# Recommendation tower on one core: a shallower order for the first chunks, and the pair spread of a group one chunk sooner

## The chip, the core and the metric

The kernel runs on one core of a Trainium2 chip. The metric is device time in microseconds (us) of one execution. The engines are TensorE (PE, matrix products), VectorE (DVE), ScalarE (ACT), GpSimd (POOL, here the issuer of the table gathers) and SyncE (SP, here the issuer of loads). Each runs its own list of instructions strictly in the written order; they meet through semaphores.

## What is computed

```python
e = stack([tbl_f[ids[:, f]] for f in range(26)], axis=1)      # 512 x 26 x 64, gathered rows
x = layer_norm(dense_t @ Wd.T)                                 # 512 x 128
y = layer_norm(einsum('bnd,ed->bne', e, Ws))                   # per field, over 128
y = layer_norm(einsum('bne,pn->bep', y, Wsi))                  # 26 fields -> 32, over 32
T = concat([x[:, None, :], swapaxes(y, 1, 2)], axis=1)         # 33 vectors of 128
Z = einsum('bnd,bmd->bnm', T, T)[:, TRIL_I, TRIL_J]            # 528 pair products
z = layer_norm(Z @ Wl.T) * mask                                # 512, 384 live
h = relu(concat([z, r_dense_t]) @ W_top1 + b_top1)
h = relu(h @ W_top2 + b_top2)
out = h @ W_top3                                               # 512 x 1
```

All of it is float32.

## The kernel before

The batch of 512 is worked in 4 groups of 128 samples, and a group in 4 chunks of 32, so 16 chunks, numbered n = 4*gp + c. A group needs 13 tiles of gathered rows: 4 in chunk c = 0 and 3 in each other. Every tile takes two indirect gathers on POOL, 104 in all, issued back to back with waits that hold POOL two chunks ahead at most.

One chunk passes through these steps (functions of the code):

1. PE `transpose_rows` writes the gathered rows, transposed, to `ps_gq`; ACT `gt_copy` brings them to SBUF; PE `gram_rows` multiplies by the Gram matrix of the embedding weight, into `ps_gq` again.
2. DVE `variance1` (multiply, reduce), ACT `deviation1` (root), DVE `scale_rows` (reciprocal, scaling of `G`): the first layer norm.
3. PE `project_fields` into `ps_ut`, ACT `ut_copy`, PE `embed` into `ps_y`, DVE `y_evacuate` (adds the bias, into `V`).
4. ACT `square2`, DVE `variance2`, ACT `deviation2`, DVE `normalise2`: the second layer norm, in `V`.
5. PE `pair_products` (16 small products into `ps_z`), ACT `z_evacuate`, DVE `z_merge` (into `zt`).

A finished group is passed on: PE `spread_pairs` (24 tiny moves from `zt` to `ps_z`), ACT `z_copy` (to `zb`, `zx`), PE `project_pairs` (5 matmuls by `wl`, into `ps_tail`), ACT `f_squares`, `deviation3`, `f_scale`, PE `transpose_features`, ACT `zn_copy`, then `layer1`, `layer2`, `layer3` with their evacuations. All of these share `ps_tail`.

The order is written by hand. `slot(n)`, one function for each engine, holds the steps of three chunks that overlap: the transposes of n, the embedding of n-1, the pair products of n-2. In a slot with c == 2, PE spreads the group before, between `gram_rows(n)` and `embed(n-1)`; the embedding of n-1 there must also wait for `normalise2(n-2)`, whose reciprocals lie in the same bank. Chunks 0 to 2 are written out one by one, and from chunk 3 on `slot` runs up to chunk 14. Chunk 15 and the end have an order of their own.

Weight preparation that needs the engines is placed among the first chunks: `prepare_dense` (the dense part of the first top layer, 4 pieces of 2 matmuls), `prepare_b1` (12 matmuls with one column each, for the bias of that layer), `prepare_xsum`, `prepare_last_block` (5 matmuls that complete `wl`), `prepare_means` and `prepare_gains` (ACT passes over `wl`). SP loads `w1d` at once, `w1z` after the gathers of chunk 0, the two parts of `wl` after those of chunks 1 and 2.

Of the kernel before, what the change touches and what calls it, by code (L numbers as in the profile page):

```python
# [31 lines left out]
P = 128  # L32
# [11 lines left out]
DENSE_ORDER = (0, 1, 3, 2)  # L44
# [3 lines left out]
NG = B // GRAN  # L48
# [43 lines left out]
def dlrm_tower(nc, ids_base, table, ws_t, gs_row, ident, small, pair_mask, merge_mask, wsi_rows, span_mask, wsi_small,  # L92
               bs_rep, wd_t, dense_t, wl_blocks, w1_z, w1_d, w2, out):
    with ExitStack() as ctx:
# [3 lines left out]
        def sem(name):  # L98
# [99 lines left out]
         b1_ps, b1_ready, dense_ps, dense_sb, dense_ready, w1_ready, last_in_ready, last_ps, last_mean, last_ready, wl_mean, wl_shift, wl_ready) = [  # L198
# [3 lines left out]
                "x_sd_ready", "x_root", "x_ready", "xsum_ps", "xsum_ready", "b1_ps", "b1_ready", "dense_ps", "dense_sb", "dense_ready",  # L202
# [22 lines left out]
        dense_banks = (ps_tail[:, :], ps_z[:, 1, :])  # L225
# [63 lines left out]
        def _(sp):  # L289
# [51 lines left out]
        def _(act):  # L341
# [9 lines left out]
            def prepare_embedding():  # L351

                act.wait_ge(wc_nat_ps, 1)
                act.copy(wc_nat[:, :], ps_ut[:, 0, 0:P]).then_inc(wc_nat_sb, 1)
                act.wait_ge(bias_ps, 1)
                act.copy(bias_y[:, :], ps_y[:, 0, 0:NPROJ]).then_inc(bias_ready, 1)

            def prepare_x():

                act.wait_ge(xc_ps, 1)  # L360
                act.activation(x_sq[:, :], ps_y[:, 1, :], ACT.Square).then_inc(x_sq_ready, 1)
                act.wait_ge(xvar_ps, 1)
# [14 lines left out]
            def dense_copy(oc):  # L377
                act.wait_ge(dense_ps, DENSE_ORDER.index(oc) + 1)
                act.copy(h1_dense[:, oc, :], dense_banks[oc % 2]).then_inc(dense_sb, 1)

            def dense_bias(oc):

                act.wait_ge(b1_ready, 1)
                act.wait_ge(dense_sb, DENSE_ORDER.index(oc) + 1)
                act.activation(h1_dense[:, oc, :], h1_dense[:, oc, :], ACT.Identity, bias=b1e[:, oc:oc + 1]).then_inc(dense_ready, 1)

            def dense_direct(oc):

                act.wait_ge(dense_ps, DENSE_ORDER.index(oc) + 1)
                act.activation(h1_dense[:, oc, :], dense_banks[oc % 2], ACT.Identity,  # L390
                               bias=b1e[:, oc:oc + 1]).then_inc(dense_sb, 1)
# [131 lines left out]

            def slot(n):
# [5 lines left out]
                if c == 3 and gp > 0:  # L530
# [10 lines left out]
                if c == 2 and gp > 0:  # L541
                    z_copy(gp - 1)
                if c == 3 and gp > 0:
                    f_scale(gp - 1)
                if n == 3:
                    prepare_means(0)
                if n == 4:
                    prepare_gains((0, 1))
# [3 lines left out]
                if c == 1 and gp > 1:  # L552
                    relu2(gp - 2)
                if c == 3 and gp > 0:
# [4 lines left out]
                if c == 1 and gp > 1:  # L559
                    y_copy(gp - 2)  # L560
                if n == 3:
                    prepare_means(1)
                    prepare_last_block()
                if n == 4:
                    prepare_gains((2, 3))
                if n == 5:
                    dense_direct(2)
# [823 lines left out]
```

## Time and profile before

| | us |
|---|---|
| median of 3 runs | 172.6 (172.5 to 173.32) |
| span of the profiled execution, first to last instruction | 170.8 |
| around the span (median less span) | 1.8 |
| PE busy | 149.1 (87%) |
| DVE busy | 125.9 (74%) |
| ACT busy | 82.9 (49%) |
| POOL busy | 100.9 (59%) |

The profiled execution's own time is taken as the median, since only its span is on the page. Busy time is a sum over the whole span. A timeline row gives the start, the duration, the engine, the line of the code, what is written and read, how many instructions were merged, and in brackets the idle time before. Merged matmul rows overlap the next by about 0.1 us, since ends are modelled: the distance of two starts is the safer measure. A float32 matmul is two passes, so `x4` is two matmuls as written.

### The profile page before, as it was taken

Reading aid. Unit: us, or ns where it says so; the run is one execution under the profiler, and the core shown is the slowest. Engines: PE = TensorE matmul, PEld = TensorE weight load, DVE = VectorE, ACT = ScalarE, POOL = GpSimd, SP = SyncE. Lnnn points to the kernel's source line nnn. Section 1 sums busy time; section 2 is a strip of 40 time slices with the busy share of each in tenths; the row PEclk is TensorE's granted clock in tenths of the full one; section 3 lists DMA queues with packets and bytes.
Section 4 is the critical chain, followed back from the end, with each engine's and each line's share of the span. In section 5 each row is a group of like instructions: output and inputs, shape, how many; then the busy total and the mean of one; then the engine's idle time right before and its main releaser. Section 6 shows DMA issues by size and latency. Waiting matters only on the chain.

```text
span 170.8 us, 3523 instructions
## 1 busy us (share of the span) xinstructions
PE 149.1 (87%) x1382; PEld 107.6 (63%) x1382; DVE 125.9 (74%) x262; ACT 82.9 (49%) x220; POOL 100.9 (59%) x109
## 2 busy tenths in 40 slices
PE   0489769997959797999999899999989999898995
PEld 0324458945535656556977565687867566687994
DVE  6596728979819795886599998496998987991044
ACT  3012333328776828776636555553637454552220
POOL 1777777777777777777777777777777200120000
PEclk9999998589996999999999999999999999999999
DMA  4913542615111111111111111111111000000000
GB/s 93 343 24 58 206 124 53 205 37 148 23 31 29 31 25 28 30 23 34 24 27 30 23 31 29 29 25 27 33 23 34 16 0 4 0 4 0 4 0 0
DMA packets 5728, 8.14 MB, mean 48 GB/s; under 512 B 2357, under 2 KB 3279, under 8 KB 5712
## 3 DMA queue, kind: packets, MB, share of 16 engines
q0 software_dynamic: 3328, 3.41, 10.9%
q1 hardware_dynamic: 1664, 3.65, 7.2%
q10 hardware_dynamic: 720, 0.85, 1.5%
q8 instruction: 11, 0.18, 0.5%
q14 instruction: 5, 0.04, 0.1%
HBM read 7.91 MB, written 0.00 MB: 46 GB/s over the span
## 4 chain that ended last, share of the span: by engine, by line
PE 50%; DVE 17%; ACT 12%; POOL 11%; issue 6%; DMA 3%; DVEq 0%
POOL G L331 11%; PE ps_tail L1106 8%; PE ps_y L1057 6%; PE ps_tail L1122 5%; PE ps_gq L1032 4%; PE ps_z L1064 4%; PE ps_ut L1044 4%; DVE V L790 4%; DVE V L774 4%; PE ps_z L1152 3%; PE ps_y L1174 3%; PE ps_tail L1016 3%; ACT sq L437 2%; DVE var L746 2%; DVE var L781 2%
## 5 line engine op out<-in xcount | busy, mean ns | idle before, releaser
L331 POOL DMA_INDIRECT G<-in_table_dram,idx x104 | 98.8, 950 | 34.7 <-issue 31.1
L1044 PE MATMUL ps_ut<-S,G 128*128 128x192 f32 (+4 forms) x128 | 21.8, 316 | 0.4 <-DVE G L760 0.4
L1044 PEld LDWEIGHTS ps_ut<-S,G 128*128 128x128 f32 x128 | 20.1, 199 | 2.0 <-DVE G L760 1.8
L774 DVE TENSOR_TENSOR V<-ps_y,bias_y 128x512 f32<-128x512 f32 x32 | 20.5, 683 | 1.0 <-PE ps_y L1057 0.9
L1064 PEld LDWEIGHTS ps_z<-V 128*64 128x64 f32 x448 | 14.9, 141 | 9.9 <-issue 5.1
L1032 PE MATMUL ps_gq<-gram,gt 128*128 128x128 f32 x104 | 15.9, 293 | 6.0 <-ACT gt L423 5.7
L1057 PE MATMUL ps_y<-ut,wcg 64*128 64x512 f32 x64 | 19.4, 684 | 1.0 <-issue 0.8
L437 ACT ACTIVATE sq<-V 128x1024 f32<-128x1024 f32 x14 | 14.9, 1062 | 10.7 <-DVE V L774 10.7
L781 DVE TENSOR_REDUCE var<-sq 128x32 f32<-128x1024 f32 x14 | 17.1, 1220 | 3.5 <-ACT sq L437 3.3
L1032 PEld LDWEIGHTS ps_gq<-gram,gt 128*128 128x128 f32 x104 | 13.5, 199 | 7.5 <-ACT gt L423 6.5
L1064 PE MATMUL ps_z<-V 128*64 128x67 f32 x448 | 16.9, 229 | 0.1
L428 ACT ACTIVATE sd<-var,eps 128x6 f32<-128x6 f32 (+1 forms) x16 | 4.8, 299 | 20.2 <-DVE var L746 20.2
L742 DVE TENSOR_TENSOR qg<-ps_gq,G 128x384 f32<-128x384 f32 (+1 forms) x16 | 9.4, 586 | 6.6 <-PE ps_gq L1032 6.6
L790 DVE TENSOR_TENSOR V<-V,ps_z 128x1024 f32<-128x1024 f32 x10 | 12.2, 1221 | 0.3
L423 ACT COPY gt<-ps_gq 128x384 f32<-128x384 f32 (+1 forms) x16 | 8.1, 509 | 7.3 <-PE ps_gq L1026 7.3
L1106 PE MATMUL ps_tail<-wl,zb 128*128 128x512 f32 x24 | 11.4, 610 | 0.0
L432 ACT COPY ut<-ps_ut 128x512 f32<-128x512 f32 x16 | 9.4, 584 | 3.2 <-PE ps_ut L1044 2.8
L832 DVE COPY_PREDICATED zt<-mmask,ps_z 128x128 f32<-128x128 int32 x28 | 7.1, 312 | 5.0 <-ACT zt L449 5.0
L337 POOL TENSOR_TENSOR V<-V,r_pool 128x1024 f32<-128x1024 f32 x1 | 1.9, 1920 | 14.7 <-DVE r_pool L796 14.7
L1026 PE MATMUL ps_gq<-eye,G 128*128 128x128 f32 x52 | 9.0, 288 | 1.8 <-DMA G<-in_table_dram,idx 1.8
L1026 PEld LDWEIGHTS ps_gq<-eye,G 128*128 128x128 f32 x52 | 6.3, 145 | 6.5 <-DMA G<-in_table_dram,idx 3.2
L746 DVE TENSOR_REDUCE var<-qg 128x6 f32<-128x384 f32 (+1 forms) x16 | 9.4, 586 | 0.6
(169 smaller groups left out, 236.6 us busy)
## 6 DMA issues: line engine op xcount, KB each, us to landing
G<-in_table_dram,idx POOLq DMA_INDIRECT x104, 2.5
w1z<-in_w_z_dram SPq DMA_DIRECT2D x1, 768.0 KB, 4.3
wl<-in_wl_blocks_dram SPq DMA_DIRECT2D x1, 768.0 KB, 5.3
dns<-in_dense_t_dram ACTq DMA_DIRECT2D x1, 512.0 KB, 4.8
w1d<-in_w_d_dram SPq DMA_DIRECT2D x1, 512.0 KB, 5.2
wl<-in_wl_blocks_dram SPq DMA_DIRECT2D x1, 512.0 KB, 3.6
w2s<-in_w_dram SPq DMA_DIRECT2D x1, 512.0 KB, 3.7
wrow<-in_wsi_rows_dram SPq DMA_DIRECT2D x1, 208.0 KB
```

The lines of the kernel that those rows point to most:

```text
L331: pool.indirect_dma_start(G[:, n // NC, j, g, :], None, table, bass.IndirectOffsetOnAxis(ap=idx[:, k:k + 1], axis=0)).then_inc(gathered[n ...
L437: act.activation(sq2[:, :, :].rearrange("p (b l) q -> p b l q", l=2), chunk_v(n), ACT.Square).then_inc(sq_ready, 1)
L746: dve.reduce_sum(var1[:, 0:2 * count], qg[:, 0:count * P].rearrange("p (t d) -> p t d", d=D), AX_X).then_inc(var1_ready, 1)
L774: dve.tensor_tensor(chunk_v(n)[:, g * CB // 2:(g + 1) * CB // 2, :, :], ps_y[:, g, :].rearrange("p (b l q) -> p b l q", l=2, q=NPROJ), bia ...
L781: dve.reduce_sum(var2[:, :], sq2[:, :, :], AX_X).then_inc(var2_ready, 1)
L790: dve.tensor_tensor(chunk_v(n), chunk_v(n), r2_at(n).rearrange("p (b l) -> p b l", l=2).unsqueeze(3).broadcast_to([P, CB, 2, NPROJ]), ALU. ...
L1026: mm = pe.transpose(ps_gq[:, i * P:(i + 1) * P], G[:, gp, j + i, :, :].rearrange("p g d -> p (g d)"), eye[:, :])
L1032: mm = pe.matmul(ps_gq[:, i * P:(i + 1) * P], gt[:, i * P:(i + 1) * P], gram[:, :], start=True, stop=True)
L1044: mm = pe.matmul(ps_ut[:, chunk % 2, col:col + width], G[:, gp, j, :, :].rearrange("p g d -> p (g d)"), S[:, j, :, :].rearrange("p s q -> ...
L1057: pe.matmul(ps_y[:, g, :], wcg[64 * g:64 * g + 64, :], ut[64 * g:64 * g + 64, :], start=True, stop=True).then_inc(y_ps, 1)
L1064: mm = pe.matmul(z_bank(n)[64 * ct:64 * ct + 64, w, s * SLOTS:(s + 1) * SLOTS], V[:, v, 3:SLOTS], V[:, v, :], start=True, stop=True)
L1106: mm = pe.matmul(ps_tail[:, :], zb[:, k, at] if k < PB else zx[:, at], wl[:, k, :], start=(k == 0), stop=(k == KB - 1))
```

## The change

On every engine chunks 0 to 3 get an order of their own, `early_slot(n)`: a chunk goes through steps 1 to 3 in its own slot rather than over two, with the second layer norm of n-1 and the pair products of n-2 beside it. Chunks 4 and 5 are written out. `prepare_b1` moves from behind the embedding of chunk 0 to ahead of the transposes of chunk 0, and the dense pieces, `prepare_xsum` and the last block (3 and 2 matmuls) lie between `gram_rows(n)` and `project_fields(n)`. The bias is added as the dense pieces leave PSUM, so three passes of `dense_bias` go. `w1z` is loaded ahead of `w1d`, and both parts of `wl` right after the gathers of chunk 0.

Group 0 is spread in chunk 4, behind the pair products of chunk 3, and projected at the end of chunk 5. Groups 1 and 2 are spread at the end of the slot with c == 1 and no longer in that with c == 2; in the slot with c == 1 the pair products of n-2 go ahead of the embedding of n-1, and DVE's `z_merge(n-2)` ahead of `variance2(n-1)`. Chunk 15 and the end are as they were.

```diff
 SP
+            sp.wait_ge(ld_x, 16)
+            sp.dma_start(w1z[:, :, :], w1_z).then_inc(ld_w1z, 16)
             sp.dma_start(w1d[:, :, :], w1_d).then_inc(ld_w1d, 16)
...
 ACT
-            def dense_copy(oc):
...
-            def dense_bias(oc):
...
+            def early_slot(n):
+                gt_copy(n)
+                square2(n - 1)
+                if n == 1:
+                    prepare_means(0)
+                else:
+                    z_evacuate(n - 2)
+                deviation1(n)
+                if n == 1:
+                    dense_direct(1)
+                    prepare_xsum()
+                if n == 2:
+                    prepare_means(1)
+                if n == 3:
+                    prepare_last_block()
+                deviation2(n - 1)
+                ut_copy(n)
+                if n == 3:
+                    prepare_gains((0, 1))
...
             def slot(n):
...
-                if c == 2 and gp > 0:
-                    z_copy(gp - 1)
...
                 deviation1(n)
+                if c == 1:
+                    z_evacuate(n - 2)
                     relu2(gp - 2)
...
                 square2(n - 1)
                 if c == 1:
-                    z_evacuate(n - 2)
                     y_copy(gp - 2)
+                    z_copy(gp - 1)
 DVE
+            def early_slot(n):
+                variance1(n)
+                if n > 1:
+                    z_merge(n - 2)
+                scale_rows(n)
+                variance2(n - 1)
+                if n == 3:
+                    prepare_shift()
+                normalise2(n - 1)
+                y_evacuate(n)
+                x_slots(n)
...
                 x_slots(n - 1)
-                variance2(n - 1)
                 if c == 1:
                     z_merge(n - 2)
+                variance2(n - 1)
...
+            variance2(3)
+            z_merge(2)
+            normalise2(3)
+            variance1(4)
+            scale_rows(4)
+            z_merge(3)
 PE
+            def early_slot(n):
+                transpose_rows(n)
+                if n > 1:
+                    pair_products(n - 2)
+                gram_rows(n)
+                if n == 1:
+                    prepare_dense(1)
+                    prepare_xsum()
+                if n == 2:
+                    prepare_last_block(range(0, 3))
+                if n == 3:
+                    prepare_last_block(range(3, KB))
+                project_fields(n)
+                embed(n)
...
             def slot(n):
...
-                if c == 2 and gp > 0:
-                    spread_pairs(gp - 1)
+                if c == 1:
+                    pair_products(n - 2)
                 embed(n - 1)
...
+                if c != 1:
+                    pair_products(n - 2)
...
+                if c == 1:
                     layer3(gp - 2)
+                    spread_pairs(gp - 1)
...
+            transpose_rows(4)
+            pair_products(2)
+            gram_rows(4)
+            prepare_dense(2)
+            pair_products(3)
+            spread_pairs(0)
+            prepare_dense(3)
+
+            transpose_rows(5)
+            project_fields(4)
+            gram_rows(5)
+            embed(4)
+            project_pairs(0)
```

On PE, chunk 13 (c == 1) before, from the Gram products of chunk 13 to those of chunk 14. `ps_y<-ut,wcg` is the embedding of chunk 12, `ps_z<-V` the pair products of chunk 11, `ps_tail<-h,sm` `layer3`, `ps_gq<-eye,G` the transposes of chunk 14, `ps_z<-zt,eye` the spread of group 2:

```order
L1032 MATMUL ps_gq<-gram,gt 128x128 x2
L1057 MATMUL ps_y<-ut,wcg 128x512 [waits y_sb,ut_sb]
L1064 MATMUL ps_z<-V 64x67 [waits z_merged,v_ready]
L1140 MATMUL ps_tail<-h,sm 1x128 [waits h2_ready]
L1026 MATMUL ps_gq<-eye,G 128x128 [waits q_used,gathered3_2]
L1044 MATMUL ps_ut<-S,G 128x192 [waits ut_sb,g_scaled]
L1032 MATMUL ps_gq<-gram,gt 128x128 [waits gt_sb]
L1152 MATMUL ps_z<-zt,eye 32x4x32 [waits z_merged]
```

The same stretch of the changed kernel:

```order
L1058 MATMUL ps_gq<-gram,gt 128x128 x2
L1090 MATMUL ps_z<-V 64x67 [waits z_merged,v_ready]
L1083 MATMUL ps_y<-ut,wcg 128x512 [waits y_sb,ut_sb]
L1168 MATMUL ps_tail<-h,sm 1x128 [waits h2_ready]
L1180 MATMUL ps_z<-zt,eye 32x4x32 [waits z_merged]
L1052 MATMUL ps_gq<-eye,G 128x128 [waits q_used,gathered3_2]
L1070 MATMUL ps_ut<-S,G 128x192 [waits ut_sb,g_scaled]
L1058 MATMUL ps_gq<-gram,gt 128x128 [waits gt_sb]
```

The pair products stand ahead of the embedding, and the spread, with its wait for the merge, ahead of the transposes, the projection and the Gram products of chunk 14.

On DVE, the changed kernel at chunks 3 to 4, from `variance2(3)` on (`sq` is `variance2`, `zt` a merge, `ps_z<-sd` and `V<-V,ps_z` `normalise2(3)`, `qg` and `var` `variance1(4)`, `G` `scale_rows(4)`, the last merge that of chunk 3, which completes group 0):

```order
L783 TENSOR_REDUCE var<-sq 128x32 [waits sq_ready]
L834 COPY_PREDICATED zt<-mmask,ps_z 128x8x16 [waits z_first]
L790 RECIPROCAL ps_z<-sd 128x32 [waits sd2_ready]
L792 TENSOR_TENSOR V<-V,ps_z 128x16x64 [waits r2_ready]
L744 TENSOR_TENSOR qg<-ps_gq,G 128x512 [waits q_ps]
L748 TENSOR_REDUCE var<-qg 128x8 [waits q_used]
L759 RECIPROCAL ps_y<-sd 128x8 [waits y_sb,sd1_ready]
L762 TENSOR_TENSOR G<-G,ps_y 128x512 [waits r1_ready]
L834 COPY_PREDICATED zt<-mmask,ps_z 128x8x16 [waits z_first]
```

The merge of chunk 3 is last in this list, and the spread of group 0 and the transposes of chunk 5 wait behind it; before, the merge of chunk 3 lay in chunk 5 and the spread in chunk 6.

## Rows read from the trace of the kernel before

**Rows 1.** The page, part 5: the gathers (busy, mean ns, idle before them).

```profile
L331 POOL DMA_INDIRECT G<-in_table_dram,idx x104 | 98.8, 950 | 34.7 <-issue 31.1
```

**Rows 2.** Timeline of POOL, the last gather (start, duration, idle before).

```profile
132.94 0.94 POOL L331 DMA_INDIRECT G<-in_table_dram,idx  x1 [0.30 <-issue]
```

**Rows 3.** Timeline of PE, transposes of chunks 1, 4, 5, 8.

```profile
22.88 0.55 PE L1026 MATMUL ps_gq<-eye,G 128*128 128x128 f32 x3 [1.64 <-DMA G<-in_table_dram,idx]
...
47.96 0.60 PE L1026 MATMUL ps_gq<-eye,G 128*128 128x128 f32 x4
...
56.25 0.55 PE L1026 MATMUL ps_gq<-eye,G 128*128 128x128 f32 x3
...
83.89 0.60 PE L1026 MATMUL ps_gq<-eye,G 128*128 128x128 f32 x4
```

**Rows 4.** Timeline of PE, chunks 13 and 14, and chunk 15's transposes.

```profile
125.27 1.13 PE L1057 MATMUL ps_y<-ut,wcg 64*128 64x512 f32 x4
126.44 1.16 PE L1064 MATMUL ps_z<-V 128*64 128x67 f32 x32
...
128.87 0.55 PE L1026 MATMUL ps_gq<-eye,G 128*128 128x128 f32 x3
129.39 1.33 PE L1044 MATMUL ps_ut<-S,G 128*128 128x192 f32 x8
...
131.61 1.41 PE L1152 MATMUL ps_z<-zt,eye 64*32 64x128 f32 x48
133.32 1.13 PE L1057 MATMUL ps_y<-ut,wcg 64*128 64x512 f32 x4 [0.29 <-issue]
...
138.14 0.49 PE L1026 MATMUL ps_gq<-eye,G 128*128 128x128 f32 x3
```

**Rows 5.** Timeline of DVE, chunk 13.

```profile
127.36 1.28 DVE L774 TENSOR_TENSOR V<-ps_y,bias_y 128x512 f32<-128x512 f32 x2
...
129.25 0.18 DVE L768 COPY V<-x_sb 128x32 f32<-128x32 f32 x1
129.77 1.22 DVE L781 TENSOR_REDUCE var<-sq 128x32 f32<-128x1024 f32 x1 [0.34 <-ACT sq L437]
130.91 0.51 DVE L832 COPY_PREDICATED zt<-mmask,ps_z 128x128 f32<-128x128 int32 x2
```

**Rows 6.** Timeline of PE: dense projection, `prepare_b1`, last block, a dense piece, `layer1`.

```profile
8.34 3.56 PE L975 MATMUL ps_y<-dns,wd 128*128 128x512 f32 x4
...
26.62 3.49 PE L988 MATMUL ps_tail<-sm,w1z 128*128 128x1 f32 x24
...
43.56 4.56 PE L1016 MATMUL ps_tail<-wl,dmat 128*128 128x512 f32 x10
...
62.31 1.98 PE L1006 MATMUL ps_tail<-dns,w1d 128*128 128x512 f32 x4
...
81.11 2.94 PE L1122 MATMUL ps_tail<-zn,w1z 128*128 128x128 f32 x24
```

**Rows 7.** The page, part 6: KB and us to landing of two loads.

```profile
w1z<-in_w_z_dram SPq DMA_DIRECT2D x1, 768.0 KB, 4.3
...
dns<-in_dense_t_dram ACTq DMA_DIRECT2D x1, 512.0 KB, 4.8
```

**Rows 8.** Windows: us, then PE, PEld, DVE, ACT, POOL busy, PEclk, DMA.

```profile
28.00:30.00 2.00, 2.00 (x14) 2.00 (x13) 1.53 (x4) 1.06 (x1) 1.70 (x2) 0.66 0.19 33
30.00:32.00 2.00, 1.82 (x8) 1.73 (x9) 1.93 (x12) 0.70 (x2) 1.39 (x3) 0.50 0.54 77
```

**Rows 9.** Timeline of DVE, scaling of chunk 15.

```profile
142.18 0.56 DVE L760 TENSOR_TENSOR G<-G,r 128x384 f32<-128x384 f32 x1
```

**Rows 10.** Timeline of ACT, `square2(12)`.

```profile
128.67 1.06 ACT L437 ACTIVATE sq<-V 128x1024 f32<-128x1024 f32 x1 [0.38 <-DVE V L774]
```

**Rows 11.** Timeline of DVE, `normalise2(2)` and `variance1(4)`'s product.

```profile
52.13 1.22 DVE L790 TENSOR_TENSOR V<-V,ps_z 128x1024 f32<-128x1024 f32 x1
53.27 0.68 DVE L742 TENSOR_TENSOR qg<-ps_gq,G 128x512 f32<-128x512 f32 x1
```

More of the change, by code:

```diff
@@ L529, in slot @@
                     deviation2(n - 2)
-                if c == 3 and gp > 0:
+                if c == 3:
                     f_squares(gp - 1)
@@ L557, in slot @@
                 if c == 1:
-                    z_evacuate(n - 2)
-                if c == 1 and gp > 1:
                     y_copy(gp - 2)
[L561 to L567, printed above, removed]
-                    prepare_gains((4,))
-                if n == 6:
-                    dense_bias(0)
-                    dense_bias(1)
-                if n == 7:
-                    dense_bias(3)
+                    z_copy(gp - 1)
             prepare_embedding()
             prepare_x()
-            dense_copy(0)
-            dense_copy(1)
             gt_copy(0)
             deviation1(0)
-            dense_copy(3)
-            gt_copy(1)
+            dense_direct(0)
             ut_copy(0)
-            deviation1(1)
-            square2(0)
-            gt_copy(2)
-            deviation2(0)
-            ut_copy(1)
-            deviation1(2)
-            square2(1)
-            prepare_xsum()
-            for n in range(3, NCHUNK - 1):
+            for n in range(1, NC):
+                early_slot(n)
+            square2(3)
+            gt_copy(4)
+            z_evacuate(2)
+            deviation2(3)
+            prepare_gains((2, 3))
+            deviation1(4)
+            z_evacuate(3)
+            dense_direct(2)
+            prepare_gains((4,))
+            z_copy(0)
+            dense_direct(3)
+            gt_copy(5)
+            ut_copy(4)
+            deviation1(5)
+            square2(4)
+            for n in range(6, NCHUNK - 1):
                 slot(n)
@@ L912, in _ @@
             prepare_x_root(1)
-            prepare_x()
+            prepare_b1()
             variance1(0)
             scale_rows(0)
+            prepare_x()
             dve.wait_ge(x_ready, 1)
             x_slots(0)
-            variance1(1)
-            dve.wait_ge(bias_ready, 1)
+            prepare_last_block()
             y_evacuate(0)
-            scale_rows(1)
-            variance2(0)
-            prepare_b1()
-            prepare_last_block()
-            for n in range(2, NCHUNK - 1):
+            for n in range(1, NC):
+                early_slot(n)
+            variance2(3)
[4 more added lines that the diff above has]
+            z_merge(3)
+            variance1(5)
+            y_evacuate(4)
+            scale_rows(5)
+            x_slots(4)
+            variance2(4)
+            for n in range(6, NCHUNK - 1):
                 slot(n)
```

104 lines of the change are left out of this document (41 added, 63 removed).

## The prediction

> **What bounds the kernel now.** I read the gathers on POOL first, then the transposes on PE against them, then one steady chunk on all engines.
>
> The 104 gathers take 950 ns each and 31.1 us of issue between 102 of them, 0.30 each, so one every 1.25 us without a real hold [rows 1]. The last one starts at 132.94 [rows 2], and with about 2.4 us from start to landing (1.0 of issue left over, estimate from chunk 1: its sixth gather, number 14, starts at 132.94 - 90 x 1.25 = 20.4, and PE goes on at 22.88 when it lands [rows 3]) chunk n's rows are there at 20.4 + 2.4 + 1.25 x (gathers behind the 14th): chunk 4 at 47.8, chunk 5 at 55.3, chunk 8 at 80.3, chunk 13 at 120.3, chunk 14 at 127.8, chunk 15 at 135.3. PE's transposes start at 47.96, 56.25, 83.89, 128.87 and 138.14 [rows 3, 4]. So up to chunk 4 the gathers pace the kernel within 0.2 us, and from there on PE is late by 1 to 4 us: it is bound by its own work and by the loop through DVE and ACT. The most that any order can win without touching the end is therefore the 2.8 us by which chunk 15 is late (138.14 against 135.3). Behind chunk 15's transposes the code is unchanged and lasts 170.8 - 138.14 = 32.7 us.
>
> In all that follows, what counts is when the transposes of a chunk start, since each slot hangs on them. I write T4 for the start of chunk 4's.
>
> **The steady slots, c == 1 and c == 2 (chunks 9, 10 and 13, 14).** Before, in chunk 13: embedding of 12 at 125.27, pair products of 11 at 126.44 (they wait for `normalise2(11)`, the embedding does not), then T14 at 128.87, projection 129.39, spread 131.61, embedding of 13 at 133.32 [rows 4]. The spread filled a time in which PE would have waited: the embedding of 13 waits for `normalise2(12)` anyway, and 0.29 of idle remains ahead of it.
>
> After, step by step:
> - The pair products still start at 126.44 (same wait), and the embedding of 12 now stands behind them: 126.44 + 1.09 = 127.53, 2.26 later than before.
> - `y_evacuate(12)` starts when the first half has left PE, 1.13 after the start of the embedding (its length in rows 4): 128.66 instead of 127.36 [rows 5], 1.3 later.
> - From its start to the end of `x_slots` 129.25 + 0.18 - 127.36 = 2.07 [rows 5], so the merge of 11, now next, can start at 130.7 and takes 0.5: the spread can start at 131.2. (That ACT has the group's last `z_evacuate` ready by then follows from the pair products ending at 127.5; in rows 5 it came only behind `variance2`.)
> - The spread takes 1.4 [rows 4], so T14 is at 132.6 instead of 128.87: +3.7.
> - From T14 to the embedding of 13 it is 133.32 - 128.87 = 4.45 [rows 4]. The spread that lay in there was cover, not cause: the path is transposes, projection, `ut_copy`, `deviation2(12)`, `normalise2(12)`. ACT does `z_copy` ahead of `gt_copy(14)`, which moves the Gram products by less than the projection hides. So the 4.45 stay, and the embedding of 13 is +3.7 too; pair products and group projection follow it at once, and T15 inherits it.
>
> This is once for group 1 (T8 to T12) and once for group 2 (T12 to T15): 2 x 3.7 = 7.4. The bounds: if the merge came at once after the pair products the spread would only move 1.4 forward and back, 0; if all of the spread and its waits came on top, 131.61 + 1.4 against 128.87 gives 4.1 each, 8.2. I take 3.7, which is a chain of named rows.
>
> **Chunk 4, written out.** From T4 to T5 it is 8.3 before (56.25 - 47.96 [rows 3]). After, T5 stands behind the spread of group 0 and a dense piece, and the spread behind the whole second layer norm of chunk 3: evacuation of 3 (0.06 + 1.28, [rows 5]), `square2(3)` 1.06 [rows 10], `variance2(3)` 1.22 and the merge of 2 about 0.5 [rows 5], `normalise2(3)` 0.38 + 1.22, `variance1(4)` 2 x 0.68 [rows 11], the root of chunk 4 0.3, `scale_rows(4)` 0.95 (estimate from 0.56 for three tiles in rows 9 and a reciprocal), the merge of 3 0.5, spread 1.4, dense piece 1.85 [rows 4, 6]: 12.0 with semaphore steps of 0.02. That is +3.7. DVE is the path here, with PE idle two times; `gt_copy(4)` is also queued behind `square2(3)` on ACT.
>
> **Chunks 5 to 7.** T5 to T8 is 27.6 before (83.89 - 56.25 [rows 3]). After: chunk 5 takes transposes 0.45, projection 1.55, Gram 0.9, embedding 1.07, group projection 4.5 (five matmuls like the last block's 4.56 [rows 6]) = 8.45. Then 4.45 to the embedding of 5, the same path as above [rows 4]. From there the loop is the evacuation 1.13 + 1.28, `square2` 1.06, `variance2` 1.22, roots and `f_squares` 1.35, `gt_copy(7)` 0.5, Gram 0.9, embedding 1.07, feature transposes 0.5, pair products 1.1, `layer1` 2.9 (the small ones are estimates, the rest is in [rows 4, 5, 6, 10]) = 13.0. Sum 25.9, so -1.7 of the possible 3.4 (spread 1.41 and dense piece 1.98 are gone from here [rows 4, 6]); the rest is lost because ACT has `f_squares` and `gt_copy(7)` behind `square2(5)`. Bounds -3.4 and 0. Chunks 4 to 7 together: +2.0.
>
> **Chunks 0 to 3.** The dense projection starts at 8.34 and lasts 3.56 [rows 6]; now it waits only for its own data, which land 4.8 us after an issue at about 2.15 [rows 7], so at 7.0: 1.3 sooner. The variance matmul ends at 12.4. `w1z` is issued at 7.0 and lands 4.3 us later [rows 7], in time. Then `prepare_b1` stands between this and T0: 3.5 us [rows 6], so T0 is near 15.9. Chunk 0 must now be embedded ahead of T1. From transposes to scaled rows takes 4.6 in chunk 15 (138.14 to 142.18 + 0.56 [rows 4, 9]); four tiles and ACT's queue make it 5.3; projection and copy 2.2, embedding 1.07: T1 at 24.5. Before it was 22.88, bound by the gathers.
>
> To this comes the clock. PE's granted clock fell to 0.66 in the stretch from 28 us and 0.50 in that from 30 us, right behind the 24 one-column passes of `prepare_b1` (26.62 for 3.49) [rows 6, 8], though PE counted as busy for 2.00 of 2.00 us. Half is 1.2 instead of 2.4 GHz. The same block now stands ahead of chunk 0's transposes, Gram products and first dense piece, on the path, where I expect the same fall: twice 0.4 + 1.1 and, of the dense piece, 0.8 beyond what DVE hides, so +2.3 and T1 at 26.8. Before, the slow stretch lay in the wait for chunk 2's and 3's gathers and cost nothing later. The bounds of this term are 0 and 3.5 (rows 6 and 8 allow all of 3.5 us of path at half speed to be doubled).
>
> The Trainium skill has, in "TensorE: Matmul & The Clock Gate", Part 1, that a monitor of how busy the array has been sets the clock, and that activity lifts the throttle. Taken by its word, a block that counts as busy should keep the clock up, and the time would be that of the second rival below; the trace speaks against it.
>
> From T1 to T4 three early slots follow. Each is one chain: 4.6 to the scaled rows, projection 1.05, `ut_copy` 0.6, embedding 1.07, 7.4 in all, and to it what ACT and DVE have ahead in their queues: the passes over `wl` ahead of `deviation1`, the last block's 3 x 0.9 us on PE ahead of `project_fields(2)` [rows 6], its evacuation ahead of `ut_copy(3)`, and `variance2(n-1)` with its root ahead of every `ut_copy(n)` (1.22 [rows 5]). I put 1.0 for these, 8.4 each, 25.2 for three; with 7.4 it would be 22.2. The gathers bring a chunk every 7.5 us, so this order gives no lead back. T4 = 26.8 + 25.2 = 52.0 against 47.96: +4.1. Bounds: T4 can't be earlier than 47.8 (-0.2).
>
> On queues: the same page says that ACT and DVE work strictly in order while PE may pull a weight load ahead. That is what makes `gt_copy(4)` wait behind `square2(3)`; no number above hangs on it beyond the rows.
>
> SP's moved loads (`wl` right behind chunk 0's gathers, 1280 KB) run beside chunk 1's gathers. Before, `w1z` did the same beside chunk 1's. I cost them at 0, up to 1 us if chunk 1's rows land late, which the later T1 hides. The three `dense_bias` passes that go from ACT cost 0.7 each in chunks 6 and 7, off the path: 0.
>
> **Sum.** +4.1 (chunks 0 to 3) + 2.0 (chunks 4 to 7) + 7.4 (groups 1 and 2) = +13.5 us on the span, 184.3; with 1.8 around it 186.1 us, against the median of 172.6.
>
> **Rivals.**
> - *The change does what it could* (faster). The early order finishes its backlog in the gathers' shadow, chunk 7 starts when its rows are there, and the moved spread lets chunks 14 and 15 do so too: T15 = 135.3, and the time 135.3 + 32.7 + 1.8 = 169.8. For it: PE is late by 1 to 4 us everywhere from chunk 5 on, and a slot c == 2 gets 1.4 us shorter on PE. Against it: DVE is busy to the last tenth in chunk 13 and the merge can't come sooner. It decides if the spread follows `layer3` with less than 0.3 us of wait. 0.11.
> - *Only the steady slots lose.* The early chunks keep T8 at 83.9, since the clock doesn't fall and the early slots take 7.5: 172.6 + 7.4 = 180.0; with the early slots as summed and only the clock kept up, 186.1 - 2.3 = 183.8. Together 0.22.
> - *The clock falls again and again.* PE idles in the new chunk 13 for 1.2 ahead of the pair products, 1.8 ahead of the spread and 1.5 ahead of the embedding of 13. A slow stretch like that at 28 to 32 us in a place where PE is the path costs up to 2 us; one for each of two groups gives 190. 0.10.
> - *Nothing comes through.* Later waits take up all shifts: 172.6 within 0.5%. Against it: chunks 13 to 15 have no slack on PE in rows 4. 0.03.
>
> The forecast, 186.1 with both the clock and the queues as above, has 0.54. Its own range is 182 to 188.
>
> A measurement of this kernel tells 0.5% (0.9 us) from no change. Faster by more 0.11, within 0.03, slower 0.86. The range, 8 in 10, takes in the second and third rival and leaves the first out: 177 to 190.
>
> **What would show it.** T1 near 26.8, T4 near 52, T5 12 us behind T4, T8 near 90; in chunks 9 and 13 an idle time of over 1 us ahead of the spread, ended by `z_merge`, and T14 over 7 us behind the embedding's place of before; granted clock 0.5 near 15 to 21 us. Wrong I am if the spread starts right behind `layer3`, or if T8 is at or before 83.9, or if slots of the early chunks take 7.5 us.

## The result and the profile after

The changed kernel takes 188.33 us (187.88 to 189.56, 4 runs) against 172.96 (172.5 to 173.53, 4 runs): ratio 1.0905, 95% interval [1.0865, 1.0945]. It is 9% slower; forecast were 186.1, in a range of 177 to 190. The profiled execution has a span of 187.8 us. It is 17.0 longer than that of before, while the medians differ by 15.4: the profiled execution, 189.56 us, is the slowest of the four, and the next part shows a reason why executions of such a kernel differ by 2 us at the start. Here and below medians and ranges are of all executions, while a ratio with its interval goes by the fast ones alone, so it can differ from the quotient of the two medians.

From the page of the changed kernel: span, busy time by engine, and PE's granted clock in 40 slices of 4.7 us:

```profile
span 187.8 us, 3522 instructions
...
PE 154.9 (83%) x1382; PEld 111.0 (59%) x1382; DVE 125.6 (67%) x262; ACT 81.6 (43%) x217; POOL 100.5 (54%) x109
...
PEclk9999999999999999987999976999999999999999
```

The work is the same (1382 matmul passes); the idle time grew by 11.2 us (21.7 to 32.9), and PE's busy time by 5.8 us for the same passes; the trace shows stretches at half clock as the reason. The line of the clock shows falls near 84, 108 and 115 us, but none at the start; that it leaves one out is seen below.

Timeline of PE in the changed kernel, the transposes of chunks 1, 4, 5, 8 and 15 (T1, T4, T5, T8, T15), which answer to [rows 3] and the last row of [rows 4]:

```profile
28.52 0.55 PE L1052 MATMUL ps_gq<-eye,G 128*128 128x128 f32 x3
...
52.78 0.66 PE L1052 MATMUL ps_gq<-eye,G 128*128 128x128 f32 x4
...
64.78 0.49 PE L1052 MATMUL ps_gq<-eye,G 128*128 128x128 f32 x3
...
91.14 0.60 PE L1052 MATMUL ps_gq<-eye,G 128*128 128x128 f32 x4
...
155.16 0.49 PE L1052 MATMUL ps_gq<-eye,G 128*128 128x128 f32 x3
```

| stretch | before | after | difference | forecast |
|---|---|---|---|---|
| start to T4 | 47.96 | 52.78 | +4.8 | +4.1 |
| T4 to T5 | 8.3 | 12.0 | +3.7 | +3.7 |
| T5 to T8 | 27.6 | 26.4 | -1.3 | -1.7 |
| T8 to T12 | 31.9 | 38.2 | +6.3 | +3.7 |
| T12 to T15 | 22.3 | 25.8 | +3.5 | +3.7 |
| T15 to the end | 32.7 | 32.6 | 0 | 0 |

(T12 starts at 115.83 before and 129.36 after.)

Timeline of PE in chunks 13 and 14 of the changed kernel, to be read against [rows 4]: pair products of 11, embedding of 12, `layer3`, spread, T14, embedding of 13.

```profile
139.97 1.16 PE L1090 MATMUL ps_z<-V 128*64 128x67 f32 x32 [1.21 <-DVE V L792]
141.06 1.13 PE L1083 MATMUL ps_y<-ut,wcg 64*128 64x512 f32 x4
142.35 0.60 PE L1168 MATMUL ps_tail<-h,sm 128*1 128x128 f32 x4 [0.16 <-ACT h L480]
144.78 1.41 PE L1180 MATMUL ps_z<-zt,eye 64*32 64x128 f32 x48 [1.83 <-DVE zt L834]
146.13 0.55 PE L1052 MATMUL ps_gq<-eye,G 128*128 128x128 f32 x3
...
150.34 1.13 PE L1083 MATMUL ps_y<-ut,wcg 64*128 64x512 f32 x4 [1.74 <-issue]
```

The two idle times are there: 1.21 ahead of the pair products, 1.83 ahead of the spread, ended by the merge (`zt`), and a third of 1.74 ahead of the embedding of 13, which [rows 4] has as 0.29. T13 to T14 takes 10.37 us instead of 6.65. The same chunk on DVE (evacuation of 12, merge of 11), against [rows 5]:

```profile
142.22 1.29 DVE L776 TENSOR_TENSOR V<-ps_y,bias_y 128x512 f32<-128x512 f32 x2 [1.25 <-PE ps_y L1083]
...
144.22 0.51 DVE L834 COPY_PREDICATED zt<-mmask,ps_z 128x128 f32<-128x128 int32 x2
```

The evacuation waits 1.25 for the embedding that was put behind, and starts 6.46 behind T13 (135.76) instead of 5.14 (127.36 - 122.22), 1.3 later; 2.0 after its start comes the merge at 144.22, and the spread 0.56 behind it. The step-by-step sum of the prediction gave these as 1.3, 2.0 and 0.5.

Chunk 4 on DVE in the changed kernel (evacuation and `variance2` of 3, `normalise2(3)`, merge of 3), and PE beside it (pair products of 3, spread of group 0):

```profile
52.88 1.29 DVE L776 TENSOR_TENSOR V<-ps_y,bias_y 128x512 f32<-128x512 f32 x2 [0.17 <-PE ps_y L1083]
...
55.29 1.22 DVE L783 TENSOR_REDUCE var<-sq 128x32 f32<-128x1024 f32 x1 [0.83 <-ACT sq L430]
...
57.30 1.22 DVE L792 TENSOR_TENSOR V<-V,ps_z 128x1024 f32<-128x1024 f32 x1
...
61.06 0.51 DVE L834 COPY_PREDICATED zt<-mmask,ps_z 128x128 f32<-128x128 int32 x2
```

```profile
58.60 1.16 PE L1090 MATMUL ps_z<-V 128*64 128x67 f32 x32
61.62 1.41 PE L1180 MATMUL ps_z<-zt,eye 64*32 64x128 f32 x48 [1.87 <-DVE zt L834]
```

DVE's chain runs from 52.88 to the merge at 61.06, with waits for ACT of 0.83 and 0.37 in it, and PE idles 1.87 for it. The spread starts 8.84 behind T4; the prediction's terms ahead of it add up to 8.83.

### The profile page after: what moved, and what is told of

It reads as the page before. It is cut to its first block, busy times and chain, and to the rows that moved or that the text cites. A ratio compares the mean times of both kernels' runs of the same rounds, so it can differ in the third digit from the quotient of the medians.

```text
span 187.8 us, 3522 instructions
## 1 busy us (share of the span) xinstructions
PE 154.9 (83%) x1382; PEld 111.0 (59%) x1382; DVE 125.6 (67%) x262; ACT 81.6 (43%) x217; POOL 100.5 (54%) x109
## 4 chain that ended last, share of the span: by engine, by line
PE 61%; DVE 19%; ACT 10%; issue 6%; DMA 2%; ACTq 1%; DVEq 0%
PE ps_y L1083 9%; PE ps_tail L1134 7%; PE ps_z L1090 6%; PE ps_gq L1058 5%; PE ps_ut L1070 5%; PE ps_tail L1150 5%; DVE V L776 4%; DVE var L783 4%; PE ps_z L1180 3%; ACT sq L430 3%; PE ps_tail L1031 3%; PE ps_gq L1052 3%; DVE V L792 3%; PE ps_tail L1012 3%; PE ps_y L1202 3%
## 5 line engine op out<-in xcount | busy, mean ns | idle before, releaser
L1070 PE MATMUL ps_ut<-S,G 128*128 128x192 f32 (+4 forms) x128 | 21.7, 315 | 1.6 <-DVE G L762 1.6
L1058 PE MATMUL ps_gq<-gram,gt 128*128 128x128 f32 x104 | 16.8, 305 | 4.7 <-ACT gt L416 4.6
L1090 PEld LDWEIGHTS ps_z<-V 128*64 128x64 f32 x448 | 15.1, 142 | 8.8 <-DVE V L792 5.1
L1058 PEld LDWEIGHTS ps_gq<-gram,gt 128*128 128x128 f32 x104 | 14.3, 209 | 5.9 <-ACT gt L416 4.6
L792 DVE TENSOR_TENSOR V<-V,ps_z 128x1024 f32<-128x1024 f32 x11 | 13.4, 1221 | 0.4
L1083 PEld LDWEIGHTS ps_y<-ut,wcg 64*128 64x128 f32 x64 | 5.1, 192 | 11.3 <-issue 7.2
L1180 PE MATMUL ps_z<-zt,eye 64*32 64x128 f32 (+1 forms) x192 | 5.7, 346 | 5.5 <-DVE zt L834 5.5
```

The costliest lines, as they stand in the source:

```text
L792: dve.tensor_tensor(chunk_v(n), chunk_v(n), r2_at(n).rearrange("p (b l) -> p b l", l=2).unsqueeze(3).broadcast_to([P, CB, 2, NPROJ]), ALU. ...
L1058: mm = pe.matmul(ps_gq[:, i * P:(i + 1) * P], gt[:, i * P:(i + 1) * P], gram[:, :], start=True, stop=True)
L1070: mm = pe.matmul(ps_ut[:, chunk % 2, col:col + width], G[:, gp, j, :, :].rearrange("p g d -> p (g d)"), S[:, j, :, :].rearrange("p s q -> ...
L1083: pe.matmul(ps_y[:, g, :], wcg[64 * g:64 * g + 64, :], ut[64 * g:64 * g + 64, :], start=True, stop=True).then_inc(y_ps, 1)
L1090: mm = pe.matmul(z_bank(n)[64 * ct:64 * ct + 64, w, s * SLOTS:(s + 1) * SLOTS], V[:, v, 3:SLOTS], V[:, v, :], start=True, stop=True)
L1180: return pe.matmul(dst[32 * q:32 * q + 32, ct, :, 32 * i:32 * i + 32], eye[half, 32 * qb:32 * qb + 32], rows, start=True, stop=True)
```

## Where the start loses: a clock that the profile doesn't always record

Timeline of PE in the changed kernel, from the dense projection to the first dense piece: projection, variance matmul, `prepare_b1`, T0, Gram products of 0, dense piece 0; then the window of 14 to 16 us (busy time of PE, PEld, DVE, ACT and POOL, then the granted clock):

```profile
6.79 3.75 PE L999 MATMUL ps_y<-dns,wd 128*128 128x512 f32 x4 [1.01 <-DMA dns<-in_dense_t_dram]
...
11.23 2.07 PE L1004 MATMUL ps_z<-x_sq,ones 128*128 128x512 f32 x2
13.10 5.12 PE L1012 MATMUL ps_tail<-sm,w1z 128*128 128x1 f32 x24
18.07 1.09 PE L1052 MATMUL ps_gq<-eye,G 128*128 128x128 f32 x4
19.94 2.05 PE L1058 MATMUL ps_gq<-gram,gt 128*128 128x128 f32 x8 [0.77 <-ACT gt L416]
21.77 3.55 PE L1031 MATMUL ps_tail<-dns,w1d 128*128 128x512 f32 x4
```

```profile
14.00:16.00 2.00, 2.00 (x11) 2.00 (x11) 1.94 (x2) 0.03 (x1) 1.62 (x2) 1.00 0.37 53
```

The granted clock reads 1.00, but the matmuls here take almost twice their time: the dense piece 3.55 us instead of 1.88, the variance matmul 2.07 instead of 1.12, T0's transposes 1.09 instead of 0.60. `prepare_b1` takes 5.12; the 3.49 of before [rows 6] was itself partly at half clock ([rows 8]: its last 2 us lie in the stretch of 0.66), and by experiment 3, where a third of it takes 0.95, the whole block at full clock would be some 2.9 (estimate). So PE ran at 1.2 GHz up to about 25 us in this execution. The dense projection is slow in every profile, that of before included: 3.42 to 3.78 us for as many passes as the dense piece does in 1.88, the record at 1.00. What differs is whether PE is faster behind it. In the profile of experiment 4, with the same code up to here, the variance matmul and `prepare_b1` are faster, and a fall of the clock is recorded while the block runs:

```profile
11.25 1.13 PE L1004 MATMUL ps_z<-x_sq,ones 128*128 128x512 f32 x2 [0.35 <-ACT x_sq L363]
12.21 3.75 PE L1012 MATMUL ps_tail<-sm,w1z 128*128 128x1 f32 x24
```

```profile
13.00:14.00 1.00, 1.00 (x10) 1.00 (x9) 0.87 (x1) 0.10 (x1) 0.69 (x2) 0.86 0.04 10
14.00:16.00 2.00, 2.00 (x11) 2.00 (x11) 2.00 (x2) 0.00 (x0) 1.57 (x2) 0.50 0.38 59
```

There T0 is at 15.82 and T1 at 26.00; in the changed kernel's profile they are at 18.07 and 28.52. The forecast was 15.9 and 26.8. (That the dense projection starts at 6.8 to 7.1 instead of 8.34 has one more reason in the code: the change also puts the small bias matmul of `prepare_bias`, which waits for DVE, behind it.) So the start costs 2.5 us more or less by the clock at which PE enters this code, at a place that is now on the path to the end. Before, that place was not on the path: all runs of the kernel before lie within 171.3 and 174.0, while three experiments that keep this start spread over 6 to 7 us and experiment 2, with the same start, over 3 (the changed kernel's own four lie within 1.7). Only one execution of each is profiled, so how much of that spread is the start isn't shown; between the two profiles above it is 2.5.

The Trainium skill, "TensorE: Matmul & The Clock Gate", Part 1, warns that the trace's clock events on this chip can be unreliable. The trace here agrees: 1.00 in the row, double durations beside it.

## Experiments

Each is compared with runs of the kernel before on the same chip: 172.8 us for experiments 1 to 4, 173.5 for 5 and 172.6 for 6 to 8. Times are medians, with the ratio's interval.

**1. The steady slots alone, in the kernel before.**

```diff
 PE, slot(n), groups 2 and 3
-                if c == 2 and gp > 0:
+                if c == 2 and gp == 1:
                     spread_pairs(gp - 1)
+                if c == 1 and gp > 1:
+                    pair_products(n - 2)
                 embed(n - 1)
...
                     layer3(gp - 2)
+                    spread_pairs(gp - 1)
 ACT
-                if c == 2 and gp > 0:
+                if c == 2 and gp == 1:
                     z_copy(gp - 1)
...
+                    z_evacuate(n - 2)      # ahead of relu2
...
+                    z_copy(gp - 1)         # behind y_copy
 DVE
+                if c == 1 and gp > 1:
+                    z_merge(n - 2)         # ahead of variance2
```

> The kernel before with only the steady part of the change, in chunks 9, 10, 13 and 14: pair products ahead of the embedding, merge ahead of variance2, spread at the end of the slot with c == 1. Theory (each move is paid where it stands, the losses add): chunk 9 to 10 and 13 to 14 take 10.4 us instead of 6.65, as in the changed kernel, so +3.7 twice less 0.2 each, +7 us: 179.6, with idle times of 1.2 and 1.8 ahead of the pair products and the spread; if the granted clock falls once as it did in group 1 of the changed kernel, 182.2. Rival (the steady slots only lose because the early order brings them late and out of step): within 1 us of before, 172.5 to 173.5.

Measured: 181.99 (181.54 to 182.8), ratio 1.0526 [1.0464, 1.0589]. T9 to T10 and T13 to T14 both take 10.36. T8 stands at 83.43, T8 to T12 takes 36.8 and T12 to T15 26.9. The windows behind the two spreads show the clock:

```profile
100.00:102.00 2.00, 2.00 (x20) 1.93 (x12) 0.00 (x0) 1.33 (x3) 1.39 (x3) 0.50 0.09 17
138.00:140.00 2.00, 2.00 (x10) 2.00 (x10) 0.00 (x0) 0.90 (x3) 0.08 (x1) 0.50 0.09 16
```

So the steady slots are paid where they stand, 3.5 a group, and with a fall of the clock in both groups 1.4 and 1.1 more. That the early order brings them out of step is refuted.

**2. The early order alone: the changed kernel with the steady slots of before.**

> The changed kernel with its steady slots (from chunk 9 on) put back to the order before; the early order stays. Theory (losses add): T8 at 91.1 as in the changed kernel, then 31.9 a group as before: 188.3 - 6.3 - 3.5 = 178.5. Rival (late and out of step): the early order is the cause of the later losses, and the time stays above 185. Second rival (PE, now late, catches up in the gathers' slack): below 176.

Measured: 177.38 (175.75 to 178.69), ratio 1.0171 [1.0099, 1.0243]. T8 at 89.62, then 31.93 for T8 to T12 and 22.31 for T12 to T15, within a hundredth what the kernel before takes. The losses add, and nothing is caught up afterwards: 4.6 for the early order and 9.2 for the slots make 13.8 of the 15.4. By the ratios it is 3.0 and 9.1. So 1.6 to 3.6 of the whole stays open, where this kernel's own runs differ by 2.9. Part of what they differ by is the clock again: in this profile it fell behind the spread of group 0, where PE had idled 1.87, and T4 to T5 took 13.6 instead of 12.0.

**3. A third of `prepare_b1`.** Its loop over k runs once, so two thirds of that bias sum are missing.

```diff
                 for oc in range(OC1):
-                    for k in range(LLIVE):
+                    for k in range(1):
...
```

> The changed kernel with 4 of the 12 one-column matmuls of prepare_b1 (two thirds of the sum for the first layer's bias are left out). In the changed kernel they take 5.0 us from 13.1 and stand ahead of chunk 0's transposes. Theory (this block and the slow PE behind it are the path until chunk 4): T0 comes 3.3 us sooner, T4 too, and the end 3.3 us, 185.0; up to 1 more if PE runs at full speed sooner. Rival (the gathers or DVE's reciprocals of x set T0 and chunk 0's chain): T0 is at 17.5 or so and the time falls by less than 1.

Measured: 185.58 (183.16 to 190.04); with such a spread the median says little, the trace more:

```profile
11.99 0.95 PE L1012 MATMUL ps_tail<-sm,w1z 128*128 128x1 f32 x8
15.13 1.08 PE L1052 MATMUL ps_gq<-eye,G 128*128 128x128 f32 x4 [2.19 <-DMA G<-in_table_dram,idx]
```

The block took 0.95 us, and then PE waited 2.19 for the gathers of chunk 0: T0 can't be before 15.1. Against 18.07 that is 2.9 sooner, but against the execution of experiment 4 (15.82) only 0.7. T4 is at 49.55, T8 at 86.41. So what `prepare_b1` costs ahead of T0 depends on the clock at which PE enters it: some 2.9 where PE is slow from the start (a third of the 5.12 would end at 14.8 there, still ahead of the gathers; estimate), and where it isn't, the gathers hide all but 0.7. Both theories were half right. The Gram products behind it still took 2.05, and the clock fell at the same place as with the whole block, though the third had ended at 12.94 and PE stood idle:

```profile
13.00:14.00 1.00, 0.00 (x0) 0.00 (x0) 1.00 (x1) 0.00 (x0) 0.70 (x2) 0.65 0.17 33
```

In all three profiles that record a fall at this start (experiments 2, 3 and 4) it comes between 13 and 14 us. That speaks against the one-column passes as its cause; what the cause is stays open.

**4. The idle time ahead of the spread filled, in the changed kernel.**

```diff
-            def layer3(gp):
+            def layer3(gp, times=1):
...
-                for k in range(OC2):
+                for k in list(range(OC2)) * times:
...
                 if c == 1:
-                    layer3(gp - 2)
+                    layer3(gp - 2, 4)
                     spread_pairs(gp - 1)
```

> The changed kernel with layer3 issued four times over in chunks 9 and 13 (1.5 us more of PE work with the same result), which fills most of the 1.82 us in which PE idles ahead of the spread. Theory (that idle time costs nothing by itself, and with it filled the granted clock doesn't fall in group 1, where the changed kernel lost 2.6 us): 188.3 - 2.6 = 185.7, chunk 9 to 10 still 10.4. Rival (the clock falls for another reason, or by chance of phase): 188.3 or a fall at another place. Rival (PE work is the bound): +1.5 twice, 191.

Measured: 185.34 (182.98 to 189.18), ratio 1.0704 [1.0596, 1.0813]. `layer3`, spread of group 1 and the embedding of 9:

```profile
100.35 1.91 PE L1168 MATMUL ps_tail<-h,sm 128*1 128x128 f32 x16 [0.16 <-ACT h L480]
102.77 1.41 PE L1180 MATMUL ps_z<-zt,eye 64*32 64x128 f32 x48 [0.52 <-DVE zt L834]
...
108.32 1.13 PE L1083 MATMUL ps_y<-ut,wcg 64*128 64x512 f32 x4 [1.74 <-issue]
```

```profile
PEclk9995799999999999789999999999999999999999
```

1.3 us more of PE work cost nothing: T9 to T10 takes 10.36. The idle time ahead of the spread is 0.52, and no slice of group 1 or 2 shows a fall. T8 to T12 takes 35.4, where the changed kernel took 38.2. This is one execution, the fastest of the four (182.98 us); the slowest, not profiled, took 6.2 more. Of the 6.6 us by which its span is shorter than the changed kernel's, 2.8 lie in group 1 and 2.5 ahead of T4, so the two times alone don't tell what the filling is worth. The changed kernel's windows in group 1:

```profile
108.00:110.00 2.00, 2.00 (x8) 2.00 (x9) 0.00 (x0) 1.32 (x3) 1.62 (x2) 0.50 0.16 32
114.00:116.00 2.00, 2.00 (x24) 1.13 (x22) 1.39 (x3) 0.30 (x1) 1.40 (x2) 0.50 0.13 25
```

**5. The same filling with the slots alone,** to tell cause from chance (experiment 1 with the `layer3` of experiment 4).

> The kernel before with the steady part of the change, as in the first of these experiments (span 179.7, T8 to T12 36.8 us, T12 to T15 26.9, granted clock down to 0.7 in both groups), and layer3 issued four times over in chunks 9 and 13, which fills the idle time ahead of the spread with 1.5 us of PE work of the same result. Theory (the two idle times of a slot let the granted clock fall, and that is what the groups lose beyond 3.5 each): no fall in the two groups, T8 to T12 35.4 and T12 to T15 25.8 as in the changed kernel with the same filling, the end 2.5 sooner, 179.5. Rival (the filled kernel of before kept its clock by chance of phase): the fall stays, 182; rival (PE work is the bound): 185.

Measured: 179.8 (179.51 to 182.2), ratio 1.0411 [1.0323, 1.0499].

```profile
PEclk9999998799999999999999978999999999999999
```

The embedding of 9, and the window behind it:

```profile
103.68 1.13 PE L1061 MATMUL ps_y<-ut,wcg 64*128 64x512 f32 x4 [1.74 <-issue]
```

```profile
105.00:107.00 2.00, 2.00 (x33) 1.87 (x28) 1.86 (x5) 0.87 (x1) 1.60 (x2) 0.50 0.22 40
```

Group 2 behaved as expected: T12 to T15 takes 25.8, without a fall. Group 1 didn't: the clock fell and T8 to T12 took 37.0. It fell in another place than in experiment 1, though: there at 100 us, behind the spread, here at 105 us, behind the 1.74 of idle time ahead of the embedding, which was left unfilled. So the expectation was half wrong.

All profiles together say more than a pair of them. In the five with the spread at c == 1 and no filling (the changed kernel and experiments 1, 3, 6 and the second of 7) there are ten such spreads in groups 1 and 2, with 1.8 or 2.5 of idle time ahead: the clock fell within 1.5 us of the spread's start at six of them. In the two with the filling (0.5 of idle time) it fell at none of four. Behind the idle time ahead of the embedding (1.3 to 1.9) it fell at four of fourteen. In the four profiles with the spread at c == 2 (the kernel before, experiments 2 and 8 and the first of 7) it fell nowhere in these groups. So no fall in these groups came without an idle time of 1.6 or more just ahead of it, but the same idle time was followed by a fall at one place and not at the next, and how much of it is needed stays open.

**6. Chunk 5's transposes ahead of group 0's spread, in the changed kernel.**

```diff
 ACT
+            gt_copy(5)
+            ut_copy(4)
             z_copy(0)
             dense_direct(3)
-            gt_copy(5)
-            ut_copy(4)
...
 PE
             pair_products(3)
-            spread_pairs(0)
-            prepare_dense(3)
-
             transpose_rows(5)
             project_fields(4)
             gram_rows(5)
+            spread_pairs(0)
+            prepare_dense(3)
             embed(4)
```

> The changed kernel with chunk 5's transposes, chunk 4's projection and chunk 5's Gram products ahead of group 0's spread and the last dense piece, as the order before has it: PE works while DVE runs variance1(4), scale_rows(4) and the merge of 3. Theory (chunk 4 costs 3.7 because PE stands 1.87 ahead of the spread; the projection of 4 can't start before 8.35 behind T4 either): T5 comes 7.1 instead of 12.0 behind T4, but T6 only 0.9 sooner, the end 0.9 sooner, some 187 against 188.3. Rival (the spread's place is the whole loss of chunk 4): T6 and the end 3.7 sooner, 184.6.

Measured: 186.22 (183.64 to 190.23), ratio 1.068 [1.0563, 1.0797].

```profile
60.46 0.55 PE L1052 MATMUL ps_gq<-eye,G 128*128 128x128 f32 x3
61.97 1.63 PE L1070 MATMUL ps_ut<-S,G 128*128 128x160 f32 x10 [0.97 <-DVE G L762]
...
72.97 0.49 PE L1052 MATMUL ps_gq<-eye,G 128*128 128x128 f32 x3
```

T5 is 6.9 behind T4 (53.55), T6 19.4 instead of the 20.0 of the changed kernel and of experiments 3 and 4. The projection of 4 waits 0.97 for DVE's scaling and starts 8.42 behind T4, where 8.35 was expected. So moving the spread back alone wins 0.6 in T4 to T6, and there the rival's 3.7 is refuted: most of chunk 4's loss is DVE's chain with all of PE's work hung behind it, not one place in PE's list. The whole time can't decide this: the runs spread over 6.6 us, and two of the four, 183.6 and 184.9, are as short as the rival had it.

**7. The exchange alone, and the spread alone, in the kernel before.** Of experiment 1's edit, first only `pair_products` ahead of `embed` with its evacuation and merge, the spread left in c == 2:

> The kernel before with only the exchange in the slots with c == 1 of groups 2 and 3: pair products ahead of the embedding, z_merge ahead of variance2; the spread stays in c == 2. Theory: the embedding of 12 comes 2.3 later, the evacuation behind it 1.3, the scaled rows of 13 too, and the path through the projection of 13 loses 1.25 a group: 172.8 + 2.5 = 175.3. Rival (the exchange is what makes the slot 10.4 long): 180.

Measured: 175.12 (173.95 to 175.91), ratio 1.0166 [1.0078, 1.0254]. Embedding of 12, T14 and the projection of 13:

```profile
127.59 1.13 PE L1060 MATMUL ps_y<-ut,wcg 64*128 64x512 f32 x4
...
129.41 0.55 PE L1029 MATMUL ps_gq<-eye,G 128*128 128x128 f32 x3
130.79 1.33 PE L1047 MATMUL ps_ut<-S,G 128*128 128x192 f32 x8 [0.83 <-DVE G L761]
```

T14 is 7.12 behind T13 instead of 6.65, the projection of 13 waits 0.83 for the scaled rows, and T12 to T15 takes 23.65, +1.3. Then only `spread_pairs` and `z_copy` moved:

> The kernel before with only the spread (and z_copy) moved from c == 2 to the end of the slot with c == 1 in groups 2 and 3, behind a z_merge that still follows variance2. Theory (what costs is that PE waits for a merge which DVE gives only at the end of its slot): the merge ends at 131.4 in chunk 13 of before, T14 at 132.8 instead of 128.87, +3.9 a group: 180.6, about that of both parts together. Rival (without the exchange the spread is nearly free): 173 to 175.

Measured: 182.33 (181.93 to 182.63), ratio 1.0567 [1.0477, 1.0658]. The spread of group 2:

```profile
136.27 1.41 PE L1153 MATMUL ps_z<-zt,eye 64*32 64x128 f32 x48 [2.52 <-DVE zt L833]
```

It waits 2.52 for a merge that comes behind `variance2`, and T13 to T14 takes 10.58. So the spread at the end of c == 1 costs 3.9 by itself, as expected. The time is 1.7 above the expected 180.6, since the clock fell in both groups here too: T8 to T12 takes 37.0 and T12 to T15 27.3, which is 5.1 and 5.0 more than before. The exchange shortens its wait (1.8) but costs 1.3 elsewhere, and together they cost 3.7: the exchange gives back only 0.2.

**8. A version that beats both.** The change's aim was to have less waiting among the first chunks. In the kernel before PE waited there for ACT: `gt_copy(4)` queued behind the passes over `wl`. Only these passes are moved:

```diff
 ACT, slot(n)
+                if n == 6:
+                    prepare_gains((2, 3))
+                    prepare_gains((4,))
...
-                if n == 4:
-                    prepare_gains((0, 1))
+                if n == 4:
+                    prepare_last_block()
+                if n == 5:
+                    prepare_gains((0, 1))
...
                 if n == 3:
                     prepare_means(1)
-                    prepare_last_block()
-                if n == 4:
-                    prepare_gains((2, 3))
                 if n == 5:
                     dense_direct(2)
-                    prepare_gains((4,))
```

> An attempt to beat the kernel before: only ACT's passes over wl are moved one or two chunks later (prepare_last_block behind ut_copy(3) in chunk 4, the gains in chunks 5 and 6), so that gt_copy(4) and gt_copy(5) do not queue behind them. In the kernel before PE idles 1.93 ahead of the Gram products of 4 and 0.88 ahead of those of 5, and the granted clock falls once there. Theory (PE late behind the gathers from chunk 5 on, so a gain passes to the end until chunk 14's rows bind): T8 2 to 3.5 sooner, T14 at 127.8 instead of 128.87, the end 1.1 sooner, 171.7. Rival (ACT's passes come due elsewhere): no change within 0.5.

Measured: 170.75 (170.69 to 170.92, 6 runs) against 172.6 (171.29 to 174.03, 11 runs), ratio 0.990 [0.984, 0.996]. Gram products of 4, then T5, T6, T14 and T15:

```profile
48.93 1.07 PE L1033 MATMUL ps_gq<-gram,gt 128*128 128x128 f32 x8
...
54.90 0.55 PE L1027 MATMUL ps_gq<-eye,G 128*128 128x128 f32 x3 [2.75 <-DMA G<-in_table_dram,idx]
...
62.50 0.55 PE L1027 MATMUL ps_gq<-eye,G 128*128 128x128 f32 x3 [0.87 <-DMA G<-in_table_dram,idx]
...
127.24 0.55 PE L1027 MATMUL ps_gq<-eye,G 128*128 128x128 f32 x3 [0.54 <-DMA G<-in_table_dram,idx]
...
136.28 0.49 PE L1027 MATMUL ps_gq<-eye,G 128*128 128x128 f32 x3
```

The Gram products of 4 start at 48.93 instead of 51.41, and T5 and T6 now wait for the gathers. T8 is at 81.62, 2.3 sooner; T14 waits 0.54 for its rows, as expected, and the end is 1.9 sooner, more than the 1.1 expected; 0.6 of the difference is that this profile's gathers ran that much earlier (the last one starts at 132.34 instead of 132.94). At T14 the gathers bind; T15 follows 9.04 behind it (9.27 before), without a wait for rows. One thing more went away: in the kernel before the clock was at 0.50 from 52.5 to 56 us, behind the idle time of 1.93, and the embedding of 3 took 2.08; here it takes 1.13 and no fall is recorded. How much of the gain is the idle time and how much the clock isn't separated. Four of the eleven runs of the kernel before took 171.3 to 171.5, so against its best executions the gain is some 0.6.

## Why the prediction was right

- *Steady slots, 2 x 3.7.* Right in mechanism and size: 3.72 from T13 to T14, and 3.5 a group in the end, since the 4.45 from T14 to the next embedding became 4.2. Experiments 1, 2 and 7 show it to be independent of the rest.
- *Chunk 4, +3.7.* Right in mechanism and size, up to the start of the spread (8.84 against 8.83 behind T4).
- *Chunks 5 to 7, -1.7.* Measured -1.3, with two errors that offset each other. Chunk 5 and the way to its embedding took 7.99 and 4.16, where the sum had 8.45 and 4.45. The rest took 14.21 instead of 13.0, since it holds a stretch at half clock that the sum hadn't: 1.65 for the Gram products of 7 instead of 0.94, and 1.91 for the embedding of 6 instead of 1.13.
- *Chunks 0 to 3, +4.1.* Measured +4.8, and that it came so close is partly luck. T0 was at 18.07 instead of 15.9, since PE was slow from before the variance matmul on; then the three early slots took 24.3 instead of 25.2. In the profiles of experiments 2 and 4, where T0 is at 15.9 and 15.8 as forecast, T4 is at 51.05 and 50.25, +3.1 and +2.3. The stretch at half clock from T0 to T1 was right in size: 10.5, 10.9 and 10.2 in these three profiles, where the sum had 10.9.
- *Why the clock falls there.* The prediction read it as falling right behind `prepare_b1`. By its own rows it falls inside the block ([rows 6] has it from 26.62 to 30.11, and [rows 8] 0.66 in 28 to 30 us), and PE had idled 1.64 ahead of T1 [rows 3]. In the changed code it falls between 13 and 14 us with the whole block and with a third of it. So the prediction's "the trace speaks against it" rests on a cause that isn't shown.
- *The clock's fall in the steady groups.* This was put down as a rival with a chance of 0.10 and a price of up to 2 each. It came in group 1, twice, with 2.7 in all (T8 to T12 is 38.2 against 35.4 with the idle time filled), and it is the greatest term that the sum left out: most of the 3.5 us between the forecast span of 184.3 and the measured 187.8.
- *Bound of 2.8 for any order that leaves the end alone.* Experiment 8 took 1.9 of it.
- *Rivals.* "Does what it could" fell with the waits of 1.8 for the merge. "Only the steady slots lose" is refuted by experiment 2, where the early order alone costs 4.6 (T8 at 89.62 instead of 83.89).

## What to carry to other kernels

A step that fills a wait isn't saved when it is moved ahead: its cover goes, and it brings its own wait along. Before moving it, follow what it waits for through the other engines' lists, and ask what then stands behind it. And where an engine waits for a short copy, look first at what the copying engine has queued ahead of it: moving ACT's passes over `wl` behind those copies won 1%, where a new order of everything lost 9%.

## What was not expected of the hardware

- The recorded granted clock read 1.00 from 4 to 30 us while matmuls took almost twice their time (3.55 for 1.88 us) up to some 25 us, and in every profile it read 1.00 beside a dense projection of 3.4 to 3.8 us. Durations of known matmuls are the surer sign.
- In group 1 of the changed kernel PE idled 1.2 us ahead of the pair products and 1.8 ahead of the spread, busy in between, and then the granted clock was down to 0.50 (108 to 110 us, and again 114 to 116 us behind an idle time of 1.9). Group 2, with the same idle times, kept its clock.
- PE entered the same code at about 12 us at full or at half clock in different executions, which moved T0 by 2.3 us (15.82 and 18.07).
